# A local step order, grouped projections and later value blocks in the layer-1 attention of a two-layer transformer kernel

## The chip, the cores and the metric

The kernel runs on one core of one Trainium2 chip, as one launch. The metric is device time in microseconds (us). The kernel before takes 2310.27 us (median of 3 runs, 2308.59 to 2312.89).

## What is computed

Two transformer layers on an input of 4 batches x 1024 positions x 128 features. Only layer 1's attention is touched by the change: per batch a global causal attention with latent keys and values, then a local one with a window of 32. The reference, cut to that:

```python
def global_latent_attn(x, wq, w_kv_down, w_k_up, w_v_up, wo):
    q = split_heads(x @ wq, H)                 # H = 16 heads of HD = 8, KVH = 4
    latent = x @ w_kv_down                     # LAT = 32
    k = split_heads(latent @ w_k_up, KVH)
    v = split_heads(latent @ w_v_up, KVH)
    q, k = (rope(q, BASE_G), rope(k, BASE_G))
    q, k = (qk_norm(q), qk_norm(k))
    k, v = (repeat_kv(k), repeat_kv(v))
    causal = i[:, None] >= i[None, :]
    return merge_heads(sdpa(q, k, v, causal)) @ wo

def local_gqa_attn(x, wq, wk, wv, wo):
    # the same with k = x @ wk, v = x @ wv and
    mask = (diff >= 0) & (diff < WIN)          # WIN = 32

x = x + global_latent_attn(rmsnorm(x, norm1_w), ...)
x = x + local_gqa_attn(rmsnorm(x, norm2_w), ...)
```

## The kernel before, in words

The program has four stages one after the other: layer 0's attention, layer 0's mixture of experts, layer 1's attention (`layer1_attention`) and layer 1's soft mixture. The change is in the third alone.

`layer1_attention` works in **rounds**: rounds 0 to 3 are the global attention of batches 0 to 3, rounds 4 to 7 the local one. Round -1 prepares the first, round 8 finishes the last. A round has 32 steps n (`STEPS`): 4 key heads x 8 blocks of 128 keys. Global rounds take the key blocks in the order 0, 7, 1, 6, 2, 5, 3, 4 (`G_ORDER`), so that two steps, a **pair**, are always the same amount: 5 score units and three value blocks of 1152 query columns together.

- A **score unit** (`score`, L1832) is two matmuls side by side into one of two buffers `s_ps`. Unit u waits until the exponential of unit u-2 has emptied its buffer. ScalarE takes the exponentials into `probsT` (`exponents`, L1963), one instruction a unit. GpSimd zeroes the upper triangle of the block on the diagonal (`cut_diagonal`, L1708).
- A **value block** (`weigh`, L1863) multiplies `probsT` with the values into `o_ps`. The block with the diagonal (c = 0) waits for the cut, the other (c = 1) for the exponentials. A step of key blocks 0 to 3 has both, one of 4 to 7 only c = 0. VectorE keeps `o_ps` in `outT` (`keep_output`, L2028) when a head is done.
- **Banks**: all else that TensorE does goes through two PSUM banks `x_ps`, in the order that the list in `shared_uses` sets, a step number beside each use: turning the normed input ("input"), the latents ("latent"), projections ("project", L1775, L1777, L1778), turning of query and key slots ("heads"), of the attention's output back ("back"), of the joined output ("att"), the output projection ("out", L1792). `fill_banks` fills them. In global rounds VectorE reads them, in local rounds ScalarE does, but for "back" and "out" (`read_bank`).

While round r runs, the next one, x = r + 1, is prepared: rotation (`rotate`, L2053 on VectorE and L1695 on GpSimd), squares and sums of the heads (`square_heads`, `sum_heads`), the inverse root by three Newton steps (`inverse_roots`, L2068 to L2075), scaling (`scale_heads`, L2081), then the five slot tiles in a high and a low part. The high part is made by VectorE in global rounds and by ScalarE in local ones (`high_parts`, L1949, at the steps in `HIGHS`), the low part by VectorE (`fill_slots`, L2092). All engines run strictly in the order of their program; at each step number an engine does the parts listed for it.

The order of a global pair on TensorE:

```python
score(u0); score(u1)
weigh_last_of(previous pair)     # its step n, c = 1, and its step n + 1, c = 0
score(u2); score(u3)
fill_banks(r, n); fill_banks(r, n + 1)
score(u4)
weigh(r, n, 0)
```

A local pair is score, score, two mask matmuls (L1844), the value blocks of the pair before, and the banks.

## Time and profile before

| | us |
|---|---|
| median of 3 runs | 2310.27 |
| the profiled execution | 2308.52 |
| its span | 2306.8 |
| TensorE busy in the span | 2147.4 (93%) |
| VectorE, ScalarE, GpSimd busy | 1449.5, 1210.5, 1046.8 |
| mean granted TensorE clock | 0.976 of full |

The span is the time from the first to the last instruction on the engines; 1.7 us lie around it. A busy TensorE is not TensorE at its peak: each matmul's record contains its way through the array. Layer 1's attention lies at 1479 to 2093 us of the span, and its first score at 1516.6.

### The profile page before, as it was taken

Reading aid. Unit: us, or ns where it says so; the run is one execution under the profiler, and the core shown is the slowest. Engines: PE = TensorE matmul, PEld = TensorE weight load, DVE = VectorE, ACT = ScalarE, POOL = GpSimd, SP = SyncE. Lnnn points to the kernel's source line nnn. Section 1 sums busy time; section 2 is a strip of 40 time slices with the busy share of each in tenths; the row PEclk is TensorE's granted clock in tenths of the full one; section 3 lists DMA queues with packets and bytes.
Section 4 is the critical chain, followed back from the end, with each engine's and each line's share of the span. In section 5 each row is a group of like instructions: output and inputs, shape, how many; then the busy total and the mean of one; then the engine's idle time right before and its main releaser. Section 6 shows DMA issues by size and latency. Waiting matters only on the chain. (4 is left out here: it accounts for less than half of the span.)

```text
span 2306.8 us, 41147 instructions
## 1 busy us (share of the span) xinstructions
PE 2147.4 (93%) x15812; PEld 1410.1 (61%) x15812; DVE 1449.5 (63%) x3302; ACT 1210.5 (52%) x1796; POOL 1046.8 (45%) x982
## 2 busy tenths in 40 slices
PE   6999999999999999998999999879999998888997
PEld 4555565555655565557888888634444445556777
DVE  5787757776687757773666566546555454567633
ACT  4555535554455535553333333267786876665653
POOL 2777757777577747784323232423332321110001
PEclk9999999999999999999999999889999999999999
DMA  2000000000000000021000000000000000003001
GB/s 78 1 1 1 1 1 1 1 1 1 1 1 1 2 1 1 1 47 31 1 1 1 1 1 1 1 1 1 1 1 1 1 1 1 2 8 75 1 1 37
DMA packets 36197, 18.17 MB, mean 8 GB/s; under 512 B 16666, under 2 KB 33828, under 8 KB 36004
## 3 DMA queue, kind: packets, MB, share of 16 engines
q1 hardware_dynamic: 36004, 15.54, 2.7%
q8 instruction: 128, 2.10, 0.4%
q14 instruction: 65, 0.53, 0.1%
HBM read 13.44 MB, written 2.10 MB: 7 GB/s over the span
## 5 line engine op out<-in xcount | busy, mean ns | idle before, releaser
L318 POOL TENSOR_TENSOR a_first<-a_first,a_ring 128x512 f32<-128x512 f32 (+3 forms) x352 | 558.0, 1585 | 253.7 <-PE a_o_ps L542 216.7
L1963 ACT ACTIVATE g_probsT<-g_s_ps 128x1024 f32<-128x1024 f32 (+2 forms) x448 | 369.0, 869 | 136.9 <-PE g_s_ps L1832 82.7
L676 ACT ACTIVATE a_ring<-a_st 128x768 f32<-128x768 f32 (+1 forms) x256 | 228.5, 918 | 86.0 <-PE a_st L527 84.3
L773 DVE TENSOR_REDUCE a_part_max<-a_mx 128x2 f32<-128x1024 f32 x128 | 156.5, 1223 | 131.7 <-PE a_mx L490 130.5
L796 DVE RECIPROCAL a_row_inv<-a_row_inv 128x256 f32<-128x256 f32 x128 | 218.6, 1732 | 24.0 <-ACT a_row_inv L664 24.0
L542 PE MATMUL a_o_ps<-a_ring,a_v 128*64 128x512 f32 (+3 forms) x1280 | 226.4, 474 | 1.6 <-POOL a_ring L300 1.4
L1243 ACT ACTIVATE m_silu<-m_up,m_b 128x512 f32<-128x512 f32 x160 | 109.8, 689 | 219.6 <-PE m_up L1178 218.1
L1863 PE MATMUL g_o_ps<-g_probsT,g_values 128*32 128x512 f32 (+5 forms) x2688 | 206.7, 419 | 5.2 <-POOL g_probsT L1708 5.1
L1708 POOL TENSOR_SCALAR_AFFINE_SELECT g_probsT<-g_probsT 128x512 f32<-128x512 f32 x128 | 88.4, 693 | 244.9 <-ACT g_probsT L1963 244.7
L1832 PE MATMUL g_s_ps<-g_qT,g_kT 64*128 64x512 f32 (+3 forms) x896 | 173.7, 435 | 27.4 <-ACT g_probsT L1963 21.7
L490 PE MATMUL a_mx<-a_k_hi,a_q_hi 64*128 64x512 f32 (+3 forms) x768 | 146.9, 404 | 24.6 <-DVE a_largest L780 17.1
L1100 POOL TENSOR_TENSOR m_acc<-m_acc,m_part 128x512 f32<-128x512 f32 x54 | 69.7, 1290 | 220.1 <-DVE m_part L1400 219.7
L1832 PEld LDWEIGHTS g_s_ps<-g_qT,g_kT 64*128 64x128 f32 x896 | 77.6, 188 | 140.2 <-ACT g_probsT L1963 97.8
L1192 PEld LDWEIGHTS m_down<-m_w,m_glu 128*128 128x128 f32 x1280 | 149.9, 193 | 3.7
L1192 PE MATMUL m_down<-m_w,m_glu 128*128 128x128 f32 x1280 | 149.9, 275 | 0.0
L780 DVE CUSTOM_DVE_ANT_0 a_masked<-a_mx,mask_wide,a_part_max 128x256 bf16<-128x256 f32 (+3 forms) x256 | 128.4, 548 | 28.2 <-PE a_mx L490 26.7
L542 PEld LDWEIGHTS a_o_ps<-a_ring,a_v 128*64 128x64 f32 x1280 | 80.9, 136 | 106.7 <-issue 65.4
L1388 DVE SCALAR_TENSOR_TENSOR m_glu<-m_up,m_b,m_silu 128x512 f32<-128x512 f32 x160 | 115.1, 745 | 45.6 <-ACT m_silu L1243 45.5
L527 PE MATMUL a_st<-a_q_hi,a_k_hi 64*128 64x512 f32 (+3 forms) x768 | 135.7, 346 | 0.0
L527 PE MATMUL a_st<-a_q_lo,a_k_hi 64*128 64x512 f32 (+3 forms) x768 | 135.4, 344 | 0.0
L527 PE MATMUL a_st<-a_shift,a_minus_one 64*128 64x512 f32 (+3 forms) x768 | 135.3, 343 | 0.0
L527 PE MATMUL a_st<-a_q_hi,a_k_lo 64*128 64x512 f32 (+3 forms) x768 | 135.3, 343 | 0.0
(344 smaller groups left out, 4271.1 us busy)
## 6 DMA issues: line engine op xcount, KB each, us to landing
m_w<-in_L_ffn_rw SPq DMA_DIRECT2D x2, 1024.0 KB, 8.9
s_w<-in_L_ffn_w SPq DMA_DIRECT2D x1, 2048.0 KB, 8.8
s_w<-in_L_ffn_w SPq DMA_DIRECT2D x4, 512.0 KB, 9.6
out_x<-x SPq DMA_DIRECT2D x8, 256.0 KB, 2.3
m_w<-in_L_ffn_rw SPq DMA_DIRECT2D x2, 512.0 KB, 6.5
x<-in_L_attn_x SPq DMA_DIRECT2D x2, 256.0 KB, 3.1
a_outT<-in_L_attn_w_k SPq DMA_DIRECT2D x1, 512.0 KB, 5.3
a_outT<-in_L_attn_w_q SPq DMA_DIRECT2D x1, 512.0 KB, 6.1
```

The costliest lines, as they stand in the source:

```text
L318: pool.tensor_tensor(total[:, h, q:q + w], total[:, h, q:q + w], probs_of(n, u)[:, h, off:off + w], ALU.add).then_inc(added, 1)
L490: last = pe.matmul(mx_ps[:, h, off:off + w], q_hi[m % 2][rows_of(h), i * P:(i + 1) * P], k_hi[m % 2][rows_of(h), key:key + w], start=True, ...
L527: last = pe.matmul(out[:, h, off:off + w], a[rows_of(h)], r[rows_of(h)], start=i == 0, stop=i == len(todo) - 1)
L542: last = pe.matmul(o_ps[rows_of(h), first_q:first_q + w], v_half[n // 4 % 2][:, j, head:head + A_HD], probs_of(n, u)[:, h, off:off + w], s ...
L676: act.activation(probs_of(n, u)[:, :, 0:w], st_ps[u % 2][:, :, 0:w], ACT.Exp).then_inc(exp_done, 1)
L773: last = dve.tensor_reduce(part_max[:, i, :], mx_ps[:], AX.X, ALU.max)
L780: last = dve.tensor_tensor_reduce(masked[1 - part][:, h, 0:w], mx_ps[:, h, off:off + w], g.mask_wide[:, HALF - w:HALF], 1.0, so_far, ALU.a ...
L796: dve.reciprocal(row_inv[c][:, cols], row_inv[c][:, cols]).then_inc(inv_ready, 1)
L1192: last = pe.matmul(down[u % 2][:, t * P:(t + 1) * P], glu[u % 2][h][:, t * P:(t + 1) * P], w3[:, e, h, :], start=h == 0 and t == 0, stop=h ...
L1832: last = pe.matmul(out, kT[r % 2][s // 2][rows, kb * P:(kb + 1) * P], qT[r % 2][rows, j:j + at_once, a:e], start=True, stop=True, skip_gro ...
L1863: last = pe.matmul(o_ps[place * SLOT:(place + 1) * SLOT, a:e], values[r % 2][:, kb, head_at(s, place) // GQ, :], probsT[(r * STEPS + n) % ...
L1963: act.activation(out, src.rearrange("p k (j n) -> p k j n", j=at_once), ACT.Exp, scale=float(HD) ** -0.5).then_inc(exp_done, 1)
```

## The change

Three things, all in `layer1_attention`:

1. **Local order.** In local rounds the projections of the next round go from steps 10 and 12 to 8 and 10, "att" from 8 to 12. Rotation, squares and sums go two steps earlier (11, 12, 13), GpSimd's sum of the rotation from 16 to 14. The Newton steps go from 16 to 15 (two of them) and 16 (the third). ScalarE's high parts go from steps 18 to 22 to steps 22 to 28, VectorE's low parts from 19 to 23 to 23 to 29.
2. **Grouped projections.** In the preparation of a global round the 4 matmuls of a half with `w_in` go first, into both banks, then the 4 with `w_up`. Before, the two kinds took turns, block by block.
3. **Global pairs.** Order u0, all three value blocks of the pair before (`weigh_global`), u1, u2, banks, u3, u4.

The diff, cut to its core:

```diff
--- before.py
+++ after.py
@@ -1490,7 +1490,7 @@
             steps = [(0, "heads", own, 3), (2, "back", old, 3), (4, "heads", own, 4), (6, "input", new, 0),
-                     (8, "att", old, 0), (10, "project", new, 0), (12, "project", new, 1), (14, "back", own, 0),
+                     (8, "project", new, 0), (10, "project", new, 1), (12, "att", old, 0), (14, "back", own, 0),
                      (16, "out", old, 0), (19, "back", own, 1), (24, "heads", new, 0), (26, "back", own, 2),
@@ -1722,9 +1722,9 @@
                             input_root(x)
-                        if x < ROUNDS and n == (13 if is_local(r) else 15):
+                        if x < ROUNDS and n == (11 if is_local(r) else 15):
                             rotate(x)
-                        if x < ROUNDS and n == (16 if is_local(r) else 18):
+                        if x < ROUNDS and n == (14 if is_local(r) else 18):
                             add_rotation(x)
@@ -1763,20 +1763,28 @@
-                def project(k, x, quarter):
+                def projected(k, quarter):
+                    return [(x_ps[k % 2][:, i * 256:i * 256 + 192], slice((quarter * 2 + i) * P, (quarter * 2 + i + 1) * P))
+                            for i in range(2)]
...
+                def project_local(k, x, quarter):
                     x_read(pe, "input", x, 0, quarter // 2)
-                    if not is_local(x):
-                        x_read(pe, "latent", x, 0, quarter // 2)
-                    for i in range(2):
-                        blk = quarter * 2 + i
-                        out = x_ps[k % 2][:, i * 256:i * 256 + 192]
-                        rows = slice(blk * P, (blk + 1) * P)
-                        if is_local(x):
-                            last = pe.matmul(out, normedT[:, rows], w_in[1][:], start=True, stop=True)
-                        else:
+                    for out, rows in projected(k, quarter):
+                        last = pe.matmul(out, normedT[:, rows], w_in[1][:], start=True, stop=True)
+                    last.then_inc(x_filled, 1)
...
+                def project_global(k, x, half):
...
+                    x_read(pe, "input", x, 0, half)
+                    for two in range(2):
+                        bank_free(k + two)
+                        for out, rows in projected(k + two, 2 * half + two):
                             pe.matmul(out[:, 0:D], normedT[:, rows], w_in[0][:, 0:D], start=True, stop=True)
+                    x_read(pe, "latent", x, 0, half)
+                    for two in range(2):
+                        for out, rows in projected(k + two, 2 * half + two):
                             last = pe.matmul(out[:, D:], latT[:, rows], w_up[:], start=True, stop=True)
-                    last.then_inc(x_filled, 1)
+                        last.then_inc(x_filled, 1)
@@ -1795,8 +1803,12 @@
                 def fill_banks(r, n):
-                    for k in uses_at(r, n):
+                    for k in uses_at(r, n) + uses_at(r, n + 1):
                         _, _, what, x, i, half = USES[k]
+                        if what == "project" and not is_local(x):
+                            if half == 0:
+                                project_global(k, x, i)
+                            continue
                         bank_free(k)
@@ -1805,7 +1817,7 @@
                         elif what == "project":
-                            project(k, x, 2 * i + half)
+                            project_local(k, x, 2 * i + half)
                         elif what == "back":
@@ -1867,23 +1879,22 @@
-                def weigh_last_of(r, n):
+                def weigh_global(r, n):
+                    weigh(r, n, 0)
                     weigh(r, n, 1)
...
                     units = [(m, unit) for m in (n, n + 1) for unit in range(len(units_of(r, key_block(r, m))))]
-                    for i in (0, 1):
-                        score(r, *units[i])
+                    score(r, *units[0])
                     if r or n:
-                        weigh_last_of(*((r, n - 2) if n else (r - 1, STEPS - 2)))
-                    for i in (2, 3):
+                        weigh_global(*((r, n - 2) if n else (r - 1, STEPS - 2)))
+                    for i in (1, 2):
                         score(r, *units[i])
                     fill_banks(r, n)
-                    fill_banks(r, n + 1)
-                    score(r, *units[4])
-                    weigh(r, n, 0)
+                    for i in (3, 4):
+                        score(r, *units[i])
@@ -1900,11 +1911,10 @@
                     else:
-                        weigh_last_of(late_r, late_n)
+                        weigh_global(late_r, late_n)
                     fill_banks(r, n)
-                    fill_banks(r, n + 1)
...
-                for n in range(STEPS):
...
+                for n in range(0, STEPS, 2):
                     fill_banks(-1, n)
@@ -1914,7 +1924,7 @@
                 weigh_all(ROUNDS - 1, STEPS - 1)
-                for n in range(STEPS):
+                for n in range(0, STEPS, 2):
                     fill_banks(ROUNDS, n)
@@ -1963,7 +1973,8 @@
-                HIGHS = {18: 0, 19: 1, 20: 2, 21: 3, 22: 4}
+                FIRST_HIGHS = {18: 0, 19: 1, 20: 2, 21: 3, 22: 4}
+                LOCAL_HIGHS = {22: 0, 23: 1, 24: 2, 26: 3, 28: 4}
                 for r in range(-1, ROUNDS + 1):
@@ -1978,8 +1989,9 @@
                                 read_bank(k)
-                        if not 0 <= r < BATCH and r + 1 < ROUNDS and n in HIGHS:
-                            high_parts(r + 1, HIGHS[n])
+                        highs = FIRST_HIGHS if r < 0 else LOCAL_HIGHS
+                        if not 0 <= r < BATCH and r + 1 < ROUNDS and n in highs:
+                            high_parts(r + 1, highs[n])
@@ -2062,11 +2074,13 @@
-                def inverse_roots(x):
+                def guess_roots(x):
...
                     own.did(dve.tensor_scalar(rs[:].bitcast(I32), ssq[:].bitcast(I32), -0.5, ROOT_GUESS, ALU.mult, ALU.add))
-                    for _ in range(3):
...
+                def better_roots(times):
+                    for _ in range(times):
                         own.settle()
@@ -2183,18 +2197,21 @@
                                 dve.wait_ge(zeroed, 9)
-                            if n == (13 if local else 15):
+                            if n == (11 if local else 15):
                                 rotate(x, 0)
                                 rotate(x, 1)
-                            if n == (14 if local else 16):
+                            if n == (12 if local else 16):
                                 square_heads()
-                            if n == (15 if local else 17):
+                            if n == (13 if local else 17):
                                 sum_heads()
-                            if n == (16 if local else 18):
-                                inverse_roots(x)
+                            if n == (15 if local else 18):
+                                guess_roots(x)
+                                better_roots(2 if local else 3)
+                            if local and n == 16:
+                                better_roots(1)
                             if n == (17 if local else 19):
                                 scale_heads(x)
-                            for i in ({19: (0,), 20: (1,), 21: (2,), 22: (3,), 23: (4,)} if local else
+                            for i in ({23: (0,), 24: (1,), 25: (2,), 27: (3,), 29: (4,)} if local else
                                       {21: (0,), 22: (1,), 23: (2,), 25: (3,), 27: (4,)}).get(n, ()):
```

How it moves instructions, by the order of the program on each engine. TensorE in global round 1, two pairs near the middle of a head (`g_s_ps` scores, `g_o_ps` value blocks, `g_x_ps` a bank), before:

```order
L1748 MATMUL g_x_ps<-ident,g_outT 128x128 x8
L1832 MATMUL g_s_ps<-g_qT,g_kT 128x256 x2
L1863 MATMUL g_o_ps<-g_probsT,g_values 32x512 x4
L1832 MATMUL g_s_ps<-g_qT,g_kT 128x384 x4
L1863 MATMUL g_o_ps<-g_probsT,g_values 32x512 x4
L1863 MATMUL g_o_ps<-g_probsT,g_values 32x128 x4
L1832 MATMUL g_s_ps<-g_qT,g_kT 128x512 x6
L1863 MATMUL g_o_ps<-g_probsT,g_values 32x384 x4
```

and now:

```order
L1748 MATMUL g_x_ps<-ident,g_outT 128x128 x8
L1844 MATMUL g_s_ps<-g_qT,g_kT 128x512 x2
L1844 MATMUL g_s_ps<-g_qT,g_kT 128x256 x2
L1844 MATMUL g_s_ps<-g_qT,g_kT 128x384 x2
L1875 MATMUL g_o_ps<-g_probsT,g_values 32x512 x8
L1875 MATMUL g_o_ps<-g_probsT,g_values 32x128 x4
L1844 MATMUL g_s_ps<-g_qT,g_kT 128x384 x2
L1844 MATMUL g_s_ps<-g_qT,g_kT 128x512 x8
L1875 MATMUL g_o_ps<-g_probsT,g_values 32x384 x4
```

TensorE goes to the value blocks once a pair where it went twice, and three score units in a row stand ahead of them.

VectorE in a local round, from the rotation to the sums (`g_outT` a kept output, `g_inv` and `g_att` a read of "back"), before:

```order
L2053 TENSOR_TENSOR g_part<-g_qk,g_cos 128x640 [waits g_x_read_act]
L2053 TENSOR_TENSOR g_part<-g_qk,g_sin 128x640 [waits g_x_read_act]
L2013 RECIPROCAL g_inv<-g_x_ps 128x16 [waits g_x_filled]
L2017 TENSOR_TENSOR g_att<-g_x_ps,g_inv 128x4x16 [waits a_y_kept]
L2017 TENSOR_TENSOR g_att<-g_x_ps,g_inv 128x4x16
L2056 TENSOR_TENSOR g_turned<-g_qk 128x1280
```

and now:

```order
L2065 TENSOR_TENSOR g_part<-g_qk,g_cos 128x640 [waits g_x_read_act]
L2065 TENSOR_TENSOR g_part<-g_qk,g_sin 128x640 [waits g_x_read_act]
L2040 COPY g_outT<-g_o_ps 128x512 [waits g_pv_done]
L2068 TENSOR_TENSOR g_turned<-g_qk 128x1280
L2072 TENSOR_REDUCE g_ssq<-g_turned 128x160 [waits a_y_kept]
L2074 TENSOR_SCALAR g_ssq<-g_ssq 128x160 [waits a_y_kept]
L2075 TENSOR_TENSOR g_turned<-g_part 128x640
L2025 RECIPROCAL g_inv<-g_x_ps 128x16 [waits g_x_filled]
```

The reads of "back" at steps 14 and 15 now stand behind the squares and sums.

ScalarE at the same round's end (`g_probsT` exponentials, `g_k_slots` and `g_q_slots` high parts, `g_kT` and `g_qT` reads of "heads"), before:

```order
L1963 ACTIVATE g_probsT<-g_s_ps 128x4x160 x4
L1949 ACTIVATE g_k_slots<-g_turned 128x32x8 x2
L1949 ACTIVATE g_q_slots<-g_turned 128x32x8 x2
L1963 ACTIVATE g_probsT<-g_s_ps 128x4x160 x2
L1949 ACTIVATE g_q_slots<-g_turned 128x32x8 x4
L1963 ACTIVATE g_probsT<-g_s_ps 128x4x160
```

and now:

```order
L1973 ACTIVATE g_probsT<-g_s_ps 128x4x128
L1959 ACTIVATE g_k_slots<-g_turned 128x32x8 x2
L1959 ACTIVATE g_q_slots<-g_turned 128x32x8 x2
L1973 ACTIVATE g_probsT<-g_s_ps 128x4x160 x2
L1939 ACTIVATE g_kT<-g_x_ps,g_rows_of 128x512 x2
L1959 ACTIVATE g_q_slots<-g_turned 128x32x8 x2
L1939 ACTIVATE g_kT<-g_x_ps,g_rows_of 128x512 x2
```

The high parts stand two pairs later, among the reads of the heads.

## Rows read from the trace of the kernel before

**Rows 1.** Stretches: span:length, busy us (x instructions) by engine, clock, DMA share, GB/s:
```profile
1516.60:1882.40 365.80, 344.85 (x2670) 152.55 (x2670) 197.32 (x459) 281.75 (x321) 118.86 (x147) 0.97 0.00 1
1609.60:1700.70 91.10, 86.73 (x684) 39.15 (x684) 50.85 (x118) 70.30 (x81) 29.99 (x37) 1.00 0.00 1
1700.70:1796.30 95.60, 91.25 (x686) 39.91 (x686) 50.77 (x118) 70.36 (x81) 29.99 (x37) 0.95 0.01 1
1796.30:1882.40 86.10, 81.81 (x666) 36.72 (x666) 44.40 (x94) 70.14 (x81) 27.87 (x36) 1.00 0.00 1
1882.40:2052.50 170.10, 147.70 (x1610) 97.08 (x1610) 96.29 (x227) 109.01 (x199) 26.13 (x15) 0.94 0.01 1
```

**Rows 2.** TensorE's waits, 1516 to 1882 us: total, times, longest:
```profile
PE g_s_ps L1832 <- ACT g_probsT L1963: 11.9, 21, 1.6
PE g_o_ps L1863 <- POOL g_probsT L1708: 5.1, 6, 1.5
```

**Rows 3.** Timeline of TensorE, global round 1: start, length, instruction [idle before]:
```profile
1662.43 1.07 PE L1863 MATMUL g_o_ps<-g_probsT,g_values 128*32 128x512 f32 x8
1663.43 0.62 PE L1832 MATMUL g_s_ps<-g_qT,g_kT 64*128 64x384 f32 x4
1663.97 1.28 PE L1863 MATMUL g_o_ps<-g_probsT,g_values 128*32 128x512 f32 x16
1665.19 0.79 PE L1832 MATMUL g_s_ps<-g_qT,g_kT 64*128 64x512 f32 x4
1665.91 2.05 PE L1792 MATMUL g_x_ps<-g_w_o,g_attT 128*128 128x128 f32 x16
1667.89 0.50 PE L1832 MATMUL g_s_ps<-g_qT,g_kT 64*128 64x512 f32 x2
1668.32 0.85 PE L1863 MATMUL g_o_ps<-g_probsT,g_values 128*32 128x384 f32 x8
```

**Rows 4.** Timeline of ScalarE and TensorE's weight loads in the same round:
```profile
1656.95 2.85 ACT L1963 ACTIVATE g_probsT<-g_s_ps 128x1024 f32<-128x1024 f32 x3 [1.84 <-PE g_s_ps L1832]
...
1668.43 1.02 ACT L1963 ACTIVATE g_probsT<-g_s_ps 128x1024 f32<-128x1024 f32 x1 [0.76 <-PE g_s_ps L1832]
...
1669.51 0.19 PEld L1832 LDWEIGHTS g_s_ps<-g_qT,g_kT 64*128 64x128 f32 x2 [0.22 <-ACT g_probsT L1963]
```

**Rows 5.** Timeline of TensorE, a projection half of a global round:
```profile
1646.11 0.49 PE L1777 MATMUL g_x_ps<-g_w_in,g_normedT 128*128 128x128 f32 x2
...
1646.88 0.49 PE L1777 MATMUL g_x_ps<-g_w_in,g_normedT 128*128 128x128 f32 x2
```

**Rows 6.** Timeline of TensorE, local round 5:
```profile
1953.83 1.09 PE L1748 MATMUL g_x_ps<-ident,g_att 128*128 128x128 f32 x8
1954.86 0.56 PE L1832 MATMUL g_s_ps<-g_qT,g_kT 64*128 64x320 f32 x4
...
1975.77 0.66 PE L1748 MATMUL g_x_ps<-ident,g_outT 128*128 128x128 f32 x4 [1.68 <-DVE hidden L2023]
1979.13 0.41 PE L1832 MATMUL g_s_ps<-g_qT,g_kT 64*128 64x320 f32 x2 [2.70 <-ACT g_probsT L1963]
```

**Rows 7.** Timeline of ScalarE and VectorE, local round 5:
```profile
1962.27 0.83 DVE L2053 TENSOR_TENSOR g_part<-g_qk,g_cos 128x640 f32<-128x640 f32 x1 [1.42 <-ACT g_values L1942]
...
1965.38 2.01 DVE L2056 TENSOR_TENSOR g_turned<-g_qk 128x1280 f32<-128x1280 f32 x1
...
1970.27 0.68 DVE L2028 COPY g_outT<-g_o_ps 128x512 f32<-128x512 f32 x1
...
1975.63 1.49 DVE L2081 TENSOR_TENSOR g_turned<-g_turned,g_rs 128x1280 f32<-128x1280 f32 x1
...
1977.15 0.72 ACT L1949 ACTIVATE g_k_slots<-g_turned 128x256 fp32r<-128x256 f32 x2 [5.60 <-DVE g_turned L2081]
...
1986.72 2.42 ACT L1929 ACTIVATE g_kT<-g_x_ps,g_rows_of 128x512 fp32r<-128x512 f32 x4 [0.54 <-PE g_x_ps L1748]
1989.02 1.31 ACT L1963 ACTIVATE g_probsT<-g_s_ps 128x640 f32<-128x640 f32 x2
```

## The prediction

> **What bounds the kernel now.** I read the stretches first, round by round. The four global rounds last 365.8 us and TensorE is busy in 344.9 of them, 94%; ScalarE in 281.8, 77%. The first three local rounds last 170.1 us with TensorE at 87% [rows 1]. So TensorE sets the time, but ScalarE is not far behind in global rounds, and each score unit needs ScalarE to empty a buffer. The waits say how well that works today: in all four global rounds TensorE waits 11.9 us for exponentials and 5.1 us for cuts [rows 2], a quarter of a microsecond in each of the 64 pairs. A pair takes 91.1/16 = 5.7 us on average in round 1, where the clock is full [rows 1]. The rest is read by the starts in the timelines.
>
> **Global pairs, what is saved.** From 1662.43 to 1663.43 a value block of 512 columns and the way out of it take 1.00, from 1663.97 to 1665.19 one of 640 columns takes 1.22 [rows 3]. So 128 columns cost 0.22, the 1152 of a pair in one visit 1.22 + 4 x 0.22 = 2.10, and a visit has 1.00 - 0.88 = 0.12 us beside its columns. The score unit ahead of a visit takes 0.43 (1667.89 to 1668.32), two units without one after them 0.72, or 0.36 each [rows 3], so entering costs 0.07. One visit less is 0.19 us a pair, 12 us in 64 pairs. "TensorEngine Tiling (Array Packing)" of the Trainium skill, section Key Properties, says that a change of tiling mode drains the array. By the page alone this part would be a gain; it has no price, and the 0.12 of the rows fits it. The late cuts go too, as c = 0 of step n is weighed a pair after its cut: up to 5.1 us [rows 2].
>
> **Global pairs, what it costs.** ScalarE's work needs cover, and the new order takes it. Put t = 0 at the start of u1. Its exponential starts 0.54 later (1667.89 score, 1668.43 exponential [rows 3, 4]). A single one takes 1.02; three in a row 2.85, so they follow each other at (2.85 - 1.02)/2 = 0.91. A score starts 0.06 after the exponential that frees its buffer (1668.43 + 1.02 = 1669.45, weights at 1669.51 [rows 4]). The next pair's u0 needs u3's exponential, the third in this row: 0.54 + 2 x 0.91 + 1.02 + 0.06 = 3.44. Then 0.43 for that score and 2.10 for the value blocks, and u1 comes again at 5.97. TensorE's own work would be ready sooner: u1, u2, u3, u4 and a bank of 8 transposes (1.03, 1953.83 to 1954.86 [rows 6]) end at 4 x 0.36 + 1.03 = 2.47. About 1.0 us a pair is idle, where ScalarE had work during both visits before. Three kinds of pair are a little shorter: those of key blocks 1 and 6 and of 2 and 5 have one 384-wide unit in the row, whose exponential I put at three quarters (-0.23), those of 3 and 4 a narrow u0 (-0.1). The mean is 5.82.
>
> A long bank does not fill this gap, because u3 stands behind it and u0 waits for u3's exponential: u1 and u2 (0.66 to 0.72), bank B, then 0.54 + 1.02 + 0.06 = 1.62, 0.43 and 2.10: 4.81 + B. The output projection (1.98, 1665.91 to 1667.89 [rows 3]) gives 6.8, a latent step, which I take to be alike, 6.7, a grouped projection half (2.3, below) 7.1 twice; less 0.6 for the narrower units among them, 27.1 together. A round is then 12 x 5.82 + 27.1 = 97.0 us. Round 1 took 91.1: +5.9. Round 2 took 95.6 at a clock of 0.95: +1.4. Round 3, without latents and with shorter local projections, comes by the same formulas to some 94.2 against 86.1: +8.1. Round 0 starts in a half-speed stretch and took 365.8 - 91.1 - 95.6 - 86.1 = 93.0; its first pair loses a value block at that clock, and I take 97.3: +4.3. The first local pair weighs three blocks where it weighed two: +0.8. Together **+20.5 us**, the visits and cuts saved being in it already. The cut of step n + 1 stays covered in three kinds of pair of four (u0 and the two other blocks lie ahead of it), in the fourth it may cost a tenth or two.
>
> **Grouped projections.** A block of the two kinds takes 0.77 (1646.11 to 1646.88 [rows 5]), four of them 3.1. Apart, six of the eight switches go; at a visit's 0.12 each that is 0.7, and a half takes some 2.3 to 2.4. In 6 halves of rounds 0 to 2 this is 4.3 us, and it is in the sum above. In the preparation before round 0 TensorE waits for the read of the last bank and the chain goes through it: two halves at 0.7, **-1.5 us**, between 0 and -3.
>
> **Local rounds.** Here is a stall: at 1975.77 TensorE has waited 1.68 for VectorE to read "out", and at 1979.13 it has waited 2.70 for an exponential [rows 6], which stood on ScalarE behind the high parts, which waited 5.60 for `scale_heads` [rows 7]. The clock of the three rounds is 0.94 [rows 1]. The new order in round 5, from its first score at 1939.9: the projections end a pair earlier, and VectorE's rotation, 22.4 into the round before (1962.27 [rows 7]), starts at 19.6. What lies from there to the scaling is the same work, 1975.63 - 1962.27 = 13.4 us, and one kept output (0.6) that came earlier before: scaling starts at 33.6 and ends at 35.1, before at 37.2. But the reads of "back" now stand behind squares and sums. Rotation 2.6, kept output 0.6, then 1965.38 to 1970.27 less the second read (4.3) [rows 7]: the first "back" is read by 27.6. TensorE's first "out" bank, ready at some 26.1, waits for that, **1.5 us, a new wait**. In return no high part stands before the exponentials of steps 18 to 21, so the score of step 22 goes at about 35.0 against 1979.13 - 1939.9 = 39.2. From there ScalarE is the slower: steps 22 to 31 hold 10 exponentials at 0.65 (1.31 for two), 10 high copies at 0.36 (0.72 for two), four key reads (2.42) and four query reads at the same 0.6 [rows 7], 15 us, with the waits between them until 51.2. A round took 170.1/3 = 56.7, so -5.5, three times: **-16.5 us**. Round 7 prepares nothing and stays.
>
> **The clock.** TensorE gets lighter: of 97 us in a global round some 14 are idle, where round 1 had 4.4 [rows 1]. Round 2 runs the same program as round 1 at a clock of 0.95 instead of 1.00 and takes 4.5 us more [rows 1], so the engine is near the edge here and idle time can cost twice. With full clock throughout the term is 0; if every global round paid what round 2 paid, 4 x 4.5 = +18. I take **+4 us**, the near quarter, since rounds 1 and 3 ran at 1.00 and part of a slow stretch is hidden under ScalarE. "TensorE: Matmul & The Clock Gate" of the Trainium skill, The HAM clock gate, says that the clock follows the engine's recent activity: a rule that speaks against this change, and the stalled local rounds with their 0.94 agree.
>
> **Sum.** 20.5 - 1.5 - 16.5 + 4 = +6.5 on the profiled execution's own 2308.52 us (its span 2306.8 and 1.7 around it): 2315.0. The median of the runs is 1.75 above that execution, so I predict 2316 us. A measurement of this kernel can tell 0.2%, 4.6 us, from no change.
>
> **Rivals.**
> *The chain is covered after all* (faster). If the visits saved and the early cuts decide and ScalarE's row is hidden, the global rounds gain 12 for visits, 5.1 for cuts and 4.3 for projections: 2308.5 - 16.5 - 1.5 - 21.4 = 2269. If they only come out even, 2290.5. For it: 94% busy says that TensorE is the bound. Against: the row of 3.44 us has four measured links, and would have to be under 2.5 to be hidden. Chance 0.1.
> *It cancels* (within 0.2%). If the row is 0.15 us shorter a pair than I add up (units overlap, records are a little long), 64 x 0.15 = 10 less: 2306, and 2311 with half of that. Chance 0.22.
> *ScalarE takes the local gain back* (slower). The high parts now stand among the reads of the heads. If each of them is waited for, and the late read of "back" costs 3 instead of 1.5, a local round gains 1.5 instead of 5.5: +12, 2328. It decides if the score of step 22 comes later than 37 us into its round, or the round's rest takes over 18. For: 15 us of ScalarE's work in 16. Chance 0.13.
> *The clock falls through the global rounds* (slower). With a slow stretch of 1 us in every second pair it is +32 in place of +4: 2344. It decides once the mean granted clock of rounds 0 to 3 goes below 0.93. For: 1.0 us idle in each pair. Against: rounds 1 and 3 at 1.00 with their own waits. Chance 0.1.
> *My forecast*, 2308 to 2325, has the rest, 0.45.
>
> **Numbers.** Low and high end leave the first and the last rival out, a tenth each, and take in the third: 2299 to 2334. Faster than 2305.7: the first rival and a third of the second, 0.18. Slower than 2314.9: the last two, 0.23, and a good half of my own, 0.25, make 0.48. The rest, 0.34, is within 0.2%.
>
> **What would show it.** Right: rows of exponentials with one gap a pair; TensorE's waits for exponentials in rounds 0 to 3 of 50 to 75 us where there were 11.9, and for cuts under 2; global rounds of about 97 us; no wait of 2.70 in local rounds, but about 1.5 for VectorE's `g_att` ahead of "out"; local rounds 4 to 6 of 51 us. Wrong: global rounds at or under 92, which would kill the row of exponentials as the limit; local rounds over 54; a clock in the global rounds under 0.93.

## The result and the profile after

| | before | after |
|---|---|---|
| median of the runs | 2308.59 us (2304.36 to 2312.89, 9 runs) | 2316.97 us (2313.05 to 2325.78, 9 runs) |
| ratio, 95% interval | | 1.0043 [1.0025, 1.0060] |
| the profiled execution | 2308.52 | 2315.78 |
| its span, mean granted clock | 2306.8, 0.976 | 2314.0, 0.984 |

The changed kernel is slower by 0.43%, at a higher mean clock. By the medians that is 8.4 us. The prediction was 2316 us, in a range of 2299 to 2334. The stretches of the kernel after, all four global rounds, then rounds 1, 2 and 3, then the first three local rounds together (columns as in [rows 1]):

```profile
1510.80:1906.80 396.00, 335.08 (x2660) 154.23 (x2661) 201.66 (x459) 277.73 (x321) 115.74 (x147) 0.97 0.00 1
1613.10:1712.60 99.50, 85.24 (x686) 39.47 (x686) 51.54 (x118) 69.33 (x81) 28.77 (x37) 0.98 0.00 1
1712.60:1810.40 97.80, 83.54 (x686) 39.10 (x686) 51.53 (x118) 69.28 (x81) 28.78 (x37) 1.00 0.00 1
1810.40:1906.80 96.40, 82.34 (x664) 38.28 (x665) 44.96 (x94) 69.26 (x81) 26.25 (x36) 0.98 0.00 1
1906.80:2059.60 152.80, 140.46 (x1616) 93.97 (x1616) 95.79 (x227) 107.83 (x199) 26.04 (x15) 1.00 0.01 2
```

Against [rows 1] TensorE does less in the global rounds (335.1 us busy for 344.9), and they last 396.0 us for 365.8. ScalarE's busy time hardly moves. The local rounds go the other way: 152.8 for 170.1, clock 1.00 for 0.94.

TensorE's waits in the global rounds, 1510 to 1907 us of the span, which answer to [rows 2]:

```profile
PE g_s_ps L1844 <- ACT g_probsT L1973: 58.0, 112, 1.6
PE g_o_ps L1875 <- POOL g_probsT L1708: 1.3, 3, 0.4
```

And in the local rounds, 1907 to 2059 us:

```profile
PE g_x_ps L1800 <- DVE g_att L2029: 4.7, 3, 1.6
...
PE g_s_ps L1844 <- ACT g_probsT L1973: 1.5, 5, 0.5
```

The waits for exponentials grew by 46 us (58.0 for 11.9), those for cuts fell by 4. In the local rounds the stall of [rows 6] is gone: 1.5 us of waits for exponentials in all three, and one new wait of about 1.6 a round ahead of the output projection.

One global pair on TensorE and ScalarE, round 2 (start, length, instruction, idle before; other engines and weight loads left out):

```profile
1736.56 0.50 PE L1844 MATMUL g_s_ps<-g_qT,g_kT 64*128 64x512 f32 x2 [0.52 <-ACT g_probsT L1973]
...
1736.99 2.16 PE L1875 MATMUL g_o_ps<-g_probsT,g_values 128*32 128x128 f32 x24
...
1739.08 0.73 PE L1844 MATMUL g_s_ps<-g_qT,g_kT 64*128 64x512 f32 x4
1739.62 4.20 ACT L1973 ACTIVATE g_probsT<-g_s_ps 128x1024 f32<-128x1024 f32 x5 [1.38 <-PE g_s_ps L1844]
...
1739.74 1.09 PE L1748 MATMUL g_x_ps<-ident,normed 128*128 128x128 f32 x8
...
1740.77 0.50 PE L1844 MATMUL g_s_ps<-g_qT,g_kT 64*128 64x512 f32 x2
...
1741.61 0.38 PE L1844 MATMUL g_s_ps<-g_qT,g_kT 64*128 64x256 f32 x2 [0.35 <-ACT g_probsT L1973]
...
1742.53 0.44 PE L1844 MATMUL g_s_ps<-g_qT,g_kT 64*128 64x384 f32 x2 [0.53 <-ACT g_probsT L1973]
```

In order these are u0, the three value blocks, u1 and u2, a bank, u3, u4, and the next pair's u0. ScalarE stands idle for 1.38 us while the value blocks run, then works in one row. From u1 (1739.08) to the next u0 (1742.53) are 3.45 us; from u0 to u0, 5.97.

Lengths of the rounds by their first scores, in us:

| | round 0 | 1 | 2 | 3 | three local rounds |
|---|---|---|---|---|---|
| before | 93.0 | 91.1 | 95.5 | 86.1 | 170.1 |
| after | 102.4 | 99.5 | 97.8 | 96.4 | 152.8 |

Where the 7.2 us of span came from (lengths rounded): the global rounds +30.2, the local rounds -17.3, the preparation ahead of the first score -3.2. The remaining -2.6 lies ahead of the stage and belongs to no edit: its first transposes start at 1479.4 us before and 1476.8 after, and between 1474.4 and 1479.9 in the twelve profiled executions of this study, whatever the kernel.

The preparation on TensorE, after, from the first transposes to the wait behind the projections:

```profile
1476.78 1.94 PE L1748 MATMUL g_x_ps<-ident,normed 128*128 128x128 f32 x8 [4.72 <-PEq L1084]
1478.65 3.62 PE L1763 MATMUL g_x_ps<-g_normedT,g_w_in 128*32 128x512 f32 x4
1482.20 1.46 PE L1782 MATMUL g_x_ps<-g_w_in,g_normedT 128*128 128x128 f32 x8
1483.59 1.10 PE L1786 MATMUL g_x_ps<-g_w_up,g_part 32*128 32x64 f32 x8
1485.04 1.13 PE L1782 MATMUL g_x_ps<-g_w_in,g_normedT 128*128 128x128 f32 x8 [0.35 <-ACT g_values L1952]
1486.09 1.10 PE L1786 MATMUL g_x_ps<-g_w_up,g_part 32*128 32x64 f32 x8
1503.21 1.94 PE L1748 MATMUL g_x_ps<-ident,g_k_slots 128*128 128x128 f32 x8 [16.01 <-DVE g_k_slots L2106]
```

The last `w_up` matmuls start 9.3 us behind the first transposes. A grouped half takes 1.05 + 1.03 = 2.1 us by the starts (1485.04, 1486.09, and 8 short matmuls at 1.03, as 1743.68 to 1744.71 in experiment 6 below), where four blocks of [rows 5] take 3.1.

### The profile page after: what moved, and what is told of

It reads as the page before. It is cut to its first block and busy times, and to the rows that moved or that the text cites. A ratio compares the mean times of both kernels' runs of the same rounds, so it can differ in the third digit from the quotient of the medians.

```text
span 2314.0 us, 41139 instructions
## 1 busy us (share of the span) xinstructions
PE 2124.0 (92%) x15812; PEld 1403.2 (61%) x15812; DVE 1453.1 (63%) x3302; ACT 1204.6 (52%) x1796; POOL 1042.2 (45%) x982
## 5 line engine op out<-in xcount | busy, mean ns | idle before, releaser
L1875 PE MATMUL g_o_ps<-g_probsT,g_values 128*32 128x512 f32 (+5 forms) x2688 | 192.3, 415 | 1.5 <-POOL g_probsT L1708 1.3
```

What stands on the lines that cost most here:

```text
L1875: last = pe.matmul(o_ps[place * SLOT:(place + 1) * SLOT, a:e], values[r % 2][:, kb, head_at(s, place) // GQ, :], probsT[(r * STEPS + n) % ...
```

## Experiments

Three words are used below. A visit is TensorE's going from the scores to value blocks and back. The link is the way from a score through its exponential to the next score in the same buffer. A plain pair is one without latents, projections or output projection.

Theory: the three parts act apart from each other. The global order costs time, because ScalarE's row of exponentials from u1 to the next u0 is covered by nothing; the other two save time. Rival one: the global rounds lengthened for another reason (clock, sums of many small things). Rival two: the local gain or the projections' gain exists only together with the new global order. Medians of before stand beside each run: 2307.96 for runs 1 to 4, 2308.89 for runs 5 to 8, 2308.10 for runs 9 and 10. Diffs are against the changed kernel unless they say otherwise. They are cut to the order of the global pairs; `late` is the round and step of the pair before.

### 1. The local order alone

Global pairs and projections in the order of before (the edit of `project_global`, which lets the two kinds take turns again, is not shown):

```diff
                 def weigh_global(r, n):
-                    weigh(r, n, 0)
                     weigh(r, n, 1)
                     weigh(r, n + 1, 0)
...
                     score(r, *units[0])
-                    if r or n:
-                        weigh_global(*((r, n - 2) if n else (r - 1, STEPS - 2)))
-                    for i in (1, 2):
-                        score(r, *units[i])
+                    score(r, *units[1])
+                    if late:
+                        weigh_global(*late)
+                    score(r, *units[2])
+                    score(r, *units[3])
                     fill_banks(r, n)
-                    for i in (3, 4):
-                        score(r, *units[i])
+                    score(r, *units[4])
+                    weigh(r, n, 0)
```

> The kernel before with the new local order alone. My theory (terms add up, each stands where the prediction put it): local rounds 4 to 6 of about 50 us instead of 56.7, with the wait of 1.6 for the reads of back ahead of out, and nothing else moves: 17 to 19 us less than before, about 2290. Rival (the parts need each other: the new local order gains only because TensorE comes into it from longer global rounds): under 10 us gained. Rival (ScalarE takes it back at the round's end): local rounds over 53 us, under 12 gained.

Measured: 2291.48 us, ratio 0.9927 [0.9908, 0.9945], local rounds 52.1, 50.2, 50.2 at a clock of 1.00. The local order is worth 16.5 us by itself, half a microsecond less than expected, and needs neither of the other parts. Its four global rounds, whose program is that of before, take 368.2 us where the trace of before has 365.8, so one trace places a global term only to some 2 us.

### 2. The grouped projections alone

Global pairs as in 1, the local order of before.

> The kernel before with grouped projections alone. Theory: 0.7 to 0.8 us in each of 6 halves on TensorE, 4.5 us, and 3 us in the preparation before round 0, where TensorE's clock stays at full for the shorter stretch: 7 to 8 us less, about 2301. Rival (the projection halves only move the wait to the exponentials behind them): 3 us, all of it from the preparation, 2305.5.

Measured: 2294.31 us, ratio 0.9946 [0.9932, 0.9961]: 13.7 us below before, more than expected. Its trace shows the preparation at 34.2 us (37.2 before) and the global rounds at 92.2, 92.4, 89.1 and 87.8, together 361.4 for 365.8. The two projection pairs take 5.96 and 6.04 us in place of 6.96 and 7.04, so a grouped half saves 1.0 us, not 0.7. That profiled execution, 2299.84 us, is the slowest of the kernel's runs, so the trace accounts for less than the median does.

### 3. The global order alone

Projections and local order of before, global pairs as changed.

> The kernel before with the new order of the global pairs alone. Theory: plain pairs of 5.98, 5.69, 5.73 and 5.93 us as after, the ungrouped projection halves stand in the open (4.81 + 3.1 each), global rounds of 99 us and over: 32 to 38 us more than before, about 2343. Rival (the clock is the cause, not the order of the exponentials): pairs in stretches at full clock as short as before, under 5.4 on average, and most of the loss in stretches at half clock.

Measured: 2353.02 us, ratio 1.019 [1.017, 1.021], 45.1 us over before. Direction right, size missed by 10 us. Stretches, rounds 0 to 3:

```profile
1515.10:1624.30 109.20, 91.25 (x628) 39.89 (x628) 52.87 (x129) 70.08 (x81) 29.69 (x37) 0.87 0.00 1
1624.30:1729.40 105.10, 91.02 (x684) 41.54 (x685) 51.75 (x118) 69.50 (x81) 28.75 (x37) 0.94 0.00 1
1729.40:1832.50 103.10, 88.85 (x686) 40.66 (x686) 51.85 (x118) 69.41 (x81) 28.74 (x37) 0.97 0.00 1
1832.50:1927.60 95.10, 80.98 (x666) 37.81 (x666) 44.95 (x94) 69.22 (x81) 26.31 (x36) 1.00 0.00 1
```

The plain pairs are those of the changed kernel to 0.01 us (5.98, 5.69, 5.74), and TensorE waits 57.0 us for exponentials: the rival, plain pairs under 5.4 at full clock, falls. What is extra lies in the three pairs around the projections of rounds 0 to 2, where the clock is below full: in round 2 they take 7.62, 9.46 and 7.63 us where the changed kernel has 6.62, 6.88 and 5.98. Round 3, which has no global projections behind it and a clock of 1.00, is no longer than in the changed kernel. The 1.0 us of the first of them (7.62 for 6.62) is the price of the alternating order, and the expectation had it. What it missed is the clock: rounds 0 to 2 together are 17.7 us longer than in the changed kernel, and six halves at 1.0 make only 6.0 of that.

### 4. Everything but the global order

Edit of run 1 on the global pairs alone; grouped projections and local order stay.

> The changed kernel with the global pairs in the old order: local order and grouped projections alone. Theory: the sum of the two, 25 us less than before, about 2284, with global rounds 1 and 3 of 89.5 and 86 us. Rival (they are not independent, the clock falls more often in one of them): under 20 us less.

Measured: 2279.32 us, ratio 0.9876 [0.9859, 0.9893]. Runs 1 and 2 gained 16.5 and 13.7 us, together 30.2; both at once gain 28.6. These two add, and rival two falls. The third part does not add to them: run 3's +45.1 less 16.5 and 13.7 would be +14.9, and the changed kernel is 8.4 over before. Grouping is worth more under the new global order, 16.4 us of the global rounds (412.4 in run 3, 396.0 in the changed kernel), than under the old one. The four global rounds of run 4:

```profile
1513.50:1871.30 357.80, 336.15 (x2670) 149.75 (x2670) 198.12 (x459) 281.72 (x321) 119.82 (x147) 0.98 0.00 1
```

The same span of rounds takes 396.0 us with the changed order, at 335.1 us busy and a clock of 0.97. Against this trace the order alone costs 38.2 us, and TensorE is as long busy in both. But traces of one global program differ by some 3 us, as slow stretches of the clock fall in different rounds. Lengths in us, granted clock in brackets:

| | global order | projections | round 0 | 1 | 2 | 3 | together |
|---|---|---|---|---|---|---|---|
| before | old | alternating | 93.0 (0.94) | 91.1 (1.00) | 95.5 (0.95) | 86.1 (1.00) | 365.8 |
| run 1 | old | alternating | 95.2 (0.93) | 93.0 (0.98) | 92.3 (0.98) | 87.8 (0.98) | 368.2 |
| run 2 | old | grouped | 92.2 (0.94) | 92.4 (0.96) | 89.1 (1.00) | 87.8 (0.98) | 361.4 |
| run 4 | old | grouped | 92.0 (0.94) | 89.1 (1.00) | 89.1 (1.00) | 87.6 (0.98) | 357.8 |
| run 8 | old | grouped | 92.2 (0.94) | 92.3 (0.96) | 89.3 (1.00) | 87.6 (0.98) | 361.4 |
| changed | new | grouped | 102.4 (0.93) | 99.5 (0.98) | 97.8 (1.00) | 96.4 (0.98) | 396.0 |

So the order costs 34.6 us against runs 2 and 8, which have its mean clock of 0.97, and 38.2 against run 4. In round 2, where all four run at 1.00, it costs 97.8 - 89.1 = 8.7 us; four times that is 35. Rival one falls: the clock explains at most some 3 us. Round 1 of run 2, which run 8 has at 92.3 us and 0.96 too, and run 4 at 89.1 and 1.00:

```profile
1603.30:1695.70 92.40, 88.02 (x686) 38.83 (x686) 51.02 (x118) 70.36 (x81) 29.86 (x37) 0.96 0.00 1
```

TensorE's waits in run 4's global rounds:

```profile
PE g_s_ps L1844 <- ACT g_probsT L1973: 12.3, 22, 1.6
PE g_o_ps L1875 <- POOL g_probsT L1708: 5.6, 7, 1.5
```

A pair of this order in its timeline, round 2:

```profile
1717.14 0.73 PE L1844 MATMUL g_s_ps<-g_qT,g_kT 64*128 64x512 f32 x4
...
1717.80 1.92 PE L1875 MATMUL g_o_ps<-g_probsT,g_values 128*32 128x512 f32 x16
1719.66 0.73 PE L1844 MATMUL g_s_ps<-g_qT,g_kT 64*128 64x512 f32 x4
```

u2 starts 2.52 us behind u0 with no idle time noted, although it needs u0's exponential: the visit of 1.86 us stood in front of it. An exponential frees its buffer 0.54 + 1.02 + 0.06 = 1.62 us behind its score (the single link), the second of a row 0.91 later, at 2.53 (the double link). The visit covers both.

### 5. Two scores ahead of the value blocks

```diff
                     score(r, *units[0])
-                    if r or n:
-                        weigh_global(*((r, n - 2) if n else (r - 1, STEPS - 2)))
-                    for i in (1, 2):
-                        score(r, *units[i])
+                    score(r, *units[1])
+                    if late:
+                        weigh_global(*late)
+                    score(r, *units[2])
+                    score(r, *units[3])
                     fill_banks(r, n)
-                    for i in (3, 4):
-                        score(r, *units[i])
+                    score(r, *units[4])
```

> The changed kernel, its global pairs in the order u0, u1, the three value blocks, u2, u3, banks, u4. Theory (with one visit a pair and two score buffers, only two exponentials can run under the visit, and three must stand in the open wherever the scores are put): the chain is then 0.54 + 2 x 0.91 + 1.02 + 0.06 before u1 instead of u0, a little shorter where u4 is narrow: pairs of 5.55 and 5.97 in turn, mean 5.76 against 5.83, so within 6 us of the changed kernel, and TensorE's waits for exponentials in the global rounds at 50 us or more. Rival (what costs is that only one score is ahead of the visit, so a second one mends it): 20 us or more less than the changed kernel.

Measured: 2312.31 us, ratio 1.0017 [1.0005, 1.0029]; rounds 104.3, 96.3, 95.1, 94.8, waits for exponentials 49.4 us, just under the 50 expected. A single visit costs nearly as much with two scores ahead of it as with one: the rival's 20 us are not there. Now the next pair's u1 waits for u4's exponential:

```profile
1746.15 0.73 PE L1844 MATMUL g_s_ps<-g_qT,g_kT 64*128 64x512 f32 x4
1747.77 0.50 PE L1844 MATMUL g_s_ps<-g_qT,g_kT 64*128 64x512 f32 x2 [0.89 <-ACT g_probsT L1973]
```

u4 and the next u0 are the first line, u1 the second, 1.62 us behind u4.

### 6. Half of every exponential

This kernel computes only the first half of each exponential's columns in rounds 1 to 3.

```diff
+                        if 0 < r < BATCH:
+                            out, src = out[:, :, :, 0:(e - a) // 2], src[:, :, :, 0:(e - a) // 2]
                         act.activation(out, src, ACT.Exp,
```

> The changed kernel, but in global rounds 1 to 3 each exponential takes only the first half of its columns (the rest of the probabilities is left as it was, so this part of the computation is left out). Theory (the row of three exponentials sets the pair): 0.54 + 2 x 0.49 + 0.60 + 0.06 = 2.2 us is hidden under TensorE's own work, plain pairs of 4.8 to 4.9 us, rounds 1 to 3 of 81 to 84 us instead of 98, waits for exponentials there under 8 us: some 2265 to 2275. Rival (switches of TensorE or its clock set the pair): rounds over 92.

Measured: 2293.31 us (2 runs), ratio 0.9932 [0.9909, 0.9955]; rounds 1 to 3 in 90.1, 90.2 and 86.4 us for 99.5, 97.8 and 96.4. With shorter exponentials and nothing else changed the pairs get shorter, so they are what TensorE waits for; but the gain is about half of what was expected. ScalarE's busy time in round 1 fell from 69.3 to 41.2 us, and in rounds 1 to 3 TensorE still waits 25.5 us for exponentials, where under 8 were expected:

```profile
1736.41 1.90 PE L1763 MATMUL g_x_ps<-g_normedT,g_w_in 128*32 128x512 f32 x4
1738.24 0.73 PE L1844 MATMUL g_s_ps<-g_qT,g_kT 64*128 64x512 f32 x4
1739.43 0.50 PE L1844 MATMUL g_s_ps<-g_qT,g_kT 64*128 64x512 f32 x2 [0.46 <-ACT g_probsT L1976]
1739.86 2.14 PE L1875 MATMUL g_o_ps<-g_probsT,g_values 128*32 128x384 f32 x24
1741.93 0.73 PE L1844 MATMUL g_s_ps<-g_qT,g_kT 64*128 64x512 f32 x4
1742.60 1.16 PE L1782 MATMUL g_x_ps<-g_w_in,g_normedT 128*128 128x128 f32 x8
1743.68 1.10 PE L1786 MATMUL g_x_ps<-g_w_up,g_part 32*128 32x64 f32 x8
1744.71 0.62 PE L1844 MATMUL g_s_ps<-g_qT,g_kT 64*128 64x384 f32 x4
```

Now u3 (1738.24) and the next u0 (1739.43) are 1.19 us apart: 0.54 + some 0.59 for half an exponential + 0.06. I had left out that u3 stands behind the bank, so one single exponential is always in the open: u1 and u2, bank, u3 to u0, u0, visit is 0.66 + 1.03 + 1.19 + 0.43 + 2.07 = 5.4 us for a plain pair. Seven of the twelve plain pairs of round 2 have 5.2 to 5.4, the others 4.9 to 6.1, so this account is not complete: the one of 6.13 also waits 0.5 us for cuts. The throughput of ScalarE is thus about half of the trouble; the single link left in the open is argued to be most of the other half.

### 7. The visit split, its second part late

```diff
                     score(r, *units[0])
-                    if r or n:
-                        weigh_global(*((r, n - 2) if n else (r - 1, STEPS - 2)))
-                    for i in (1, 2):
-                        score(r, *units[i])
+                    score(r, *units[1])
+                    if late:
+                        weigh(*late, 0)
+                        weigh(*late, 1)
+                    score(r, *units[2])
+                    score(r, *units[3])
                     fill_banks(r, n)
-                    for i in (3, 4):
-                        score(r, *units[i])
+                    if late:
+                        weigh(late[0], late[1] + 1, 0)
+                    score(r, *units[4])
```

> Local order and grouped projections as in the changed kernel; global pairs with two visits, but every block a pair later: u0, u1, both blocks of step n - 2, u2, u3, banks, the block of step n - 1, u4. Theory (two visits are needed to cover ScalarE; late blocks free TensorE from the cuts): as no_global, 2279, but without the 5.6 us of waits for cuts, 2270 to 2275. Rival (any block moved a pair later costs, by whatever way): over 2285.

Measured: 2303.22 us, ratio 0.9973 [0.9961, 0.9986]; rounds 98.4, 95.8, 97.4, 93.7, waits for exponentials 48.9 us, none for cuts. The expectation failed and its rival's time came out. In the timeline u4, the next u0 and the wait in front of the next u1:

```profile
1739.37 0.73 PE L1844 MATMUL g_s_ps<-g_qT,g_kT 64*128 64x512 f32 x4
1740.99 0.49 PE L1844 MATMUL g_s_ps<-g_qT,g_kT 64*128 64x512 f32 x2 [0.89 <-ACT g_probsT L1976]
```

From u4 to u1 are 1.62 us, the link of run 4, with only u0 to cover it. Two visits a pair are not enough: in this order something has to stand right behind u4.

### 8. Reads of "back" ahead of the sums in local rounds

Against run 4, to test the cause of the new local wait:

```diff
-                            if n == (13 if local else 17):
+                            if n == (15 if local else 17):
                                 sum_heads()
-                            if n == (15 if local else 18):
+                            if n == (16 if local else 18):
                                 guess_roots(x)
                                 better_roots(2 if local else 3)
-                            if local and n == 16:
+                            if local and n == 17:
                                 better_roots(1)
```

> As the kernel with local order and grouped projections and old global pairs (2279), but in local rounds the sums stand at step 15 behind both reads of back, the first two Newton steps at 16 behind the first read of out, the third at 17. Theory: the wait of 1.6 us ahead of out goes, scaling ends no later, ScalarE's row at the end of the round starts earlier: 1 to 1.5 us in each of three rounds, 3 to 4.5 less, 2275. Rival (scaling is what the round's end waits for): no change.

Measured: 2275.23 us (2269.92 to 2275.79), ratio 0.9847 [0.9830, 0.9864]; local rounds 50.1, 48.7, 48.7, together 147.4 for the 152.5 of run 4: 5.1 us less by the traces, 4.1 by the medians and 5.0 with each taken from its own before, and the rival (no change) falls. The pair with the output projection takes 3.75 us instead of 5.40. VectorE and TensorE there:

```profile
1947.67 0.36 DVE L2029 TENSOR_TENSOR g_att<-g_x_ps,g_inv 128x64 f32<-128x64 f32 x2
1947.94 1.48 DVE L2072 TENSOR_REDUCE g_ssq<-g_turned 128x160 f32<-128x1280 f32 x1
1948.41 2.05 PE L1800 MATMUL g_x_ps<-g_w_o,g_attT 128*128 128x128 f32 x16
```

Against the same place in the changed kernel, where the sum, 1.49 us long, stands in front of the reads:

```profile
1983.81 1.49 DVE L2072 TENSOR_REDUCE g_ssq<-g_turned 128x160 f32<-128x1280 f32 x1
...
1986.92 2.05 PE L1800 MATMUL g_x_ps<-g_w_o,g_attT 128*128 128x128 f32 x16 [1.58 <-DVE g_att L2029]
```

This is the fastest kernel of the study, 34 us under before and 42 under the changed one.

### 9. A short visit early, the long one behind u4

The runs so far ask for cover in two places. This order puts one value block of the pair before behind u1, and the pair's own other two behind u4 (the last argument of `weigh` only says which block ends the step's count):

```diff
                     score(r, *units[0])
-                    if r or n:
-                        weigh_global(*((r, n - 2) if n else (r - 1, STEPS - 2)))
-                    for i in (1, 2):
-                        score(r, *units[i])
+                    score(r, *units[1])
+                    if late:
+                        weigh(late[0], late[1] + 1, 0)
+                    score(r, *units[2])
+                    score(r, *units[3])
                     fill_banks(r, n)
-                    for i in (3, 4):
-                        score(r, *units[i])
+                    score(r, *units[4])
+                    weigh(r, n, 1, False)
+                    weigh(r, n, 0, True)
```

> The changed kernel with other global pairs: scores 0 and 1, then one value block of the pair before (its second step's first block), scores 2 and 3, the bank fillings, score 4, and behind it this pair's own two other value blocks. The theory (the bank of a score comes free by the row of exponentials, so a short visit has to stand behind score 1 and the long one behind score 4, where it covers the exponential that the next pair's score 1 waits for): plain pairs of about 5.1 us, rounds 1 and 2 of about 84 us each in place of 99.5 and 97.8, waits for exponentials under 30 us over the global rounds, and 2255 to 2265 us, some 20 below the 2279 measured with the order of before in the global rounds. The rival (the visits now wait for exponentials and turned sums made shortly before, or the granted clock falls with fewer matmuls at work): cuts or value waits of 0.3 us and more a pair, plain pairs no shorter than 5.5 us, and no better than 2275 us.

Measured: 2298.96 us, ratio 0.9951 [0.9933, 0.9969]; rounds 98.0, 95.4, 95.4, 93.8, plain pairs 5.57, 5.72, 5.64. The time and the pairs are the rival's, but its reason is only a part: the waits for cuts and own exponentials are 11.0 us in 64 pairs, 0.17 a pair where it asked for 0.3, and the clock is 0.98. The waits for exponentials kept to the theory's 30 us and still more than doubled against run 4 (12.3). TensorE's waits in its global rounds:

```profile
PE g_s_ps L1844 <- ACT g_probsT L1973: 28.0, 88, 1.1
PE g_o_ps L1875 <- POOL g_probsT L1708: 7.2, 17, 0.8
PE g_o_ps L1875 <- ACT g_probsT L1973: 3.8, 9, 0.5
```

and a pair, from the long visit on:

```profile
1735.31 1.71 PE L1875 MATMUL g_o_ps<-g_probsT,g_values 128*32 128x512 f32 x16
1736.95 0.73 PE L1844 MATMUL g_s_ps<-g_qT,g_kT 64*128 64x512 f32 x4
1737.62 0.64 PE L1875 MATMUL g_o_ps<-g_probsT,g_values 128*32 128x256 f32 x8
1738.57 0.50 PE L1844 MATMUL g_s_ps<-g_qT,g_kT 64*128 64x512 f32 x2 [0.32 <-ACT g_probsT L1973]
1739.48 0.44 PE L1844 MATMUL g_s_ps<-g_qT,g_kT 64*128 64x384 f32 x2 [0.42 <-ACT g_probsT L1973]
```

u2 starts 1.62 us behind u0 and u3 2.53 behind it, the two links of run 4, to the hundredth. The short visit of 0.6 us covers too little of them, which the expectation had left out, and own value blocks weighed so soon also wait for their cuts. The three kinds of wait together are 39.0 us for run 4's 17.9, 21 of the 25 us by which the global rounds are longer (382.7 for 357.8). Of the orders run here the best has the long visit behind u1 and the short one behind u4, which is the order of before.

### 10. The same with the local order of run 8

> The same with the local order in which ScalarE's read of the projections stands ahead of the squares' sums, as measured alone with the global order of before (2275, local rounds 50.1, 48.7, 48.7 us). If the two gains lie in different rounds they add: 3 to 4 us below the run without it, about 2256 us, local rounds of 50, 49 and 49 us. If the global order leaves the local rounds other clocks or late exponentials: less than 2 us below it.

Measured: 2297.06 us, ratio 0.9941 [0.9923, 0.9958], 1.9 us below run 9. The medians alone would speak for the second expectation. The traces speak for the first: the local rounds are 48.7, 48.6 and 48.6 us where run 9 has 50.6, 50.2 and 50.2, together 5.1 us less, and run 8 gained the same 5.1 against run 4. So the local edit is worth the same under either global order. What hides it in the time lies outside: this profiled execution reaches the stage's first score 6.4 us later than that of run 9 (1513.8 and 1507.4 us) and spends 1.6 us more behind the local rounds, while its global rounds happen to be 2.3 shorter (380.4 for 382.7).

## Why the prediction was right

2316 us was predicted, 2316.97 measured. The mechanisms held, but the total is closer than the terms deserve: two kinds of them were mis-sized, in opposite directions. The distance to before was also less well met than the number: predicted were 5.7 us over the 2310.27 on record, measured are 8.4 by the medians, since before itself came out 1.7 lower over nine runs, and 9.9 by the ratio.

**The global row of exponentials: right, to the hundredth.** I had 3.44 us from u1 to the next u0; the timeline shows 3.45. The plain pair with full-width units was to take 5.97 and takes 5.97, some 14 us a round were to be idle and round 2 has 14.3, waits for exponentials were to be 50 to 75 us and are 58.0, cuts under 2 and are 1.3. The mean of the four kinds of plain pair was to be 5.82; eleven of the twelve of round 2 have a mean of 5.87. What I missed is the twelfth, the round's fourth pair, 6.57 us: there one of GpSimd's cuts takes 1.47 us, the others 0.64, while VectorE squares the normed input (L2049, 1.22 us), and TensorE waits 0.43 for it. The kernel before has the same pair at 6.49 us among its shorter ones, so its trace could have told. Round 2, at full clock, took 97.8 us for 97.0.

**The sum.** The terms as predicted, and as the traces of the changed kernel and of runs 2, 4 and 8 (grouped projections under the old order) give them:

| | predicted | measured |
|---|---|---|
| global order, with the join and the clock | 20.5 + 4.3 + 4 = +28.8 | 396.0 - 361.4 or 357.8 = +34.6 to +38.2 |
| grouped projections in rounds 0 to 2 | -4.3 | 361.4 or 357.8 - 365.8 = -4.4 to -8.0 |
| preparation | -1.5 | -3.2 |
| three local rounds | -16.5 | -17.3 |
| ahead of the stage | 0 | -2.6 |
| span | +6.5 | +7.2 |

(The first two rows make +30.2 together in either case; the measured column adds to 7.1, as the lengths are rounded. The join, predicted at 0.8, is the first local pair, 0.3 longer, and stands in the local row.) The first term was 6 to 9 us too small, the next two together saved 2 to 5 us more than predicted, and 2.6 us came from nowhere in the change: the total was lucky by that much.

**The term of the global order: mis-sized in rounds 0 and 2.** Against run 4 the four rounds cost 10.4, 10.4, 8.7 and 8.8 us, against run 2 10.2, 7.1, 8.7 and 8.7; I had 5.7, 7.3, 2.8 and 8.1 before the clock's 4, where the 1.4 us of grouped projections in each of rounds 0 to 2 is added back. In round 2 I set my 97.0 against the 95.6 of before at a clock of 0.95, and let those 4.5 slow microseconds stand as part of the baseline. But they belong to that one execution: run 1, with the same global program, has rounds 1 to 3 at 0.98 each. Round 2 runs at 1.00 in runs 2, 4 and 8 (89.1 to 89.3 us) and in the changed kernel. Round 0 takes 102.4 us for the 97.3 predicted, and there the clock is most of what I missed: three pairs take 7.37, 7.46 and 7.53 us there where round 2 has 5.74, 5.97 and 5.98, and run 6, whose round 0 is the same program, repeats them to 0.01. Rounds 1 and 3 have one such pair each (8.52 for 6.88, 7.38 for 5.98). These five make 7.7 us, less what slow stretches cost the old order in the same rounds; I had 4 for it.

**Grouped projections and preparation: mis-sized.** I priced six switches at a visit's 0.12 us and got 0.7 a half. A half saves 1.0, so six save 6.0, which lies inside the -4.4 to -8.0 of the traces. In the preparation, where I had -1.5 and at most -3, the last of the grouped matmuls start 9.3 us behind the first transposes, before 13.1: from 1488.1 us on the engine ran at 1.2 GHz, half its clock, and that caught the last blocks of the alternating order (0.80 and 0.69 us a record where the blocks ahead have 0.49 and 0.43). In the changed kernel the projections are over when the slow stretch begins, at 1489.2. All nine traces with grouped projections have 33.0 to 34.2 us from the first transposes to the first score, the three with alternating ones 37.2 to 37.6. By itself the edit was worth 12.5 us by its ratio, where my two terms made 5.8; the traces of runs 2, 4 and 8 give 7.4 to 11.4 for them.

**The local order: right.** Predicted -16.5, measured -17.3, and 16.5 by the medians of run 1. The two stalls went and the new wait of 1.5 came (1.58). Run 8 shows that its cause is the one I had named, the sums ahead of the reads of "back". Rounds of 51.2 us were predicted; they are 52.3, 50.2 and 50.2. The score of step 22 was to go at 35.0 us into round 5 and goes at 35.0.

**The rule on the clock.** "TensorE: Matmul & The Clock Gate" of the Trainium skill, The HAM clock gate, says that the clock follows the engine's recent activity, which I read as speaking against this change. In the local rounds it worked for it: fewer stalls, and the clock rose from 0.94 to 1.00, also in run 1, which has the local order alone (runs 2 and 3, without it, have 0.94). In the global rounds the clock stayed at 0.97, though TensorE waited 46 us more. Nor does idle time alone tell the clock: run 3 and the changed kernel wait alike for exponentials (57.0 and 58.0 us), with clocks of 0.87, 0.94 and 0.97 in rounds 0 to 2 for alternating projections and 0.93, 0.98 and 1.00 for grouped ones, in one trace each. Under the old order grouping shows no such effect (0.97 before and in run 1; 0.97, 0.98 and 0.97 in runs 2, 4 and 8). Why it does under the new one stays open.

**The rivals.** That the row is covered after all fell with the 112 waits. That it cancels needed a row shorter by 0.15 us; it was right to 0.01. ScalarE did not take the local gain back: from the score of step 22 to the round's end are 15.2 us in all three, where 18 was the mark. The clock of the global rounds is 0.97, above the 0.93 at which the last rival was to decide.

What stays open: the median of run 2 is 13.7 us below before, and its trace shows 3.0 in the preparation, 4.4 in the global rounds and 2.5 ahead of the stage. Its profiled execution is its slowest run, and no faster one was profiled.

## What to carry to other kernels

With two score buffers, a visit of TensorE to other work is, in this kernel, less a cost than the cover of an exponential. Count for each score how much stands between it and the one that reuses its buffer (here 1.62 us for the first, 0.91 more for the next), and put the longest piece of other work where two exponentials lie in a row; putting two pieces together to save a visit of 0.1 to 0.2 us cost 35 to 38 us here. Where an edit has three parts, time each alone: two of these three gained 29 us together, and the third hid it.
